# GpSimd's small indirect DMAs are handed out tile by tile in nine stages of a graph transformer

## The chip, the cores and the metric

One NeuronCore of one Trainium2 chip runs the whole program in one launch. The metric is device time in microseconds, from several runs of the same kernel. TensorE (PE), VectorE (DVE), ScalarE (ACT) and GpSimd (POOL) compute; SyncE (SP) and GpSimd issue DMAs, which sixteen DMA engines carry out.

## The reference, cut to what matters

3125 nodes with 256 features, 100,000 edges. Two blocks of layers:

```
xn = layernorm(x)
x  = x + graph_attention_2_layers(xn, src, dst) + hyperbolic_mixer(xn)      # block 0
x  = x + routed_mlp(layernorm(x))                                           # top half of the nodes
xn = layernorm(x)
x  = x + graph_convolution(xn, src, dst) + linear_attention_4_layers(xn)    # block 1
x  = x + experts(layernorm(x))      # 4 dense MLPs, mixed by gates
```

The gates of `experts` come from a small graph attention over 65,536 edges: for each edge, a row of 20 numbers of its source node is needed, and the edges must be sorted by destination. The kernel sorts them itself by a two-pass radix sort (by the low 6 bits, then by the high bits of the destination). Each pass ends in a scatter of 65,536 words of 4 bytes to memory, 128 words to a DMA, so 512 DMAs a pass. The fetch of the rows is 537 gathers of 128 rows of 80 bytes.

## The kernel before, in words

The nodes lie as 25 tiles of 125 rows (`NT = 25`, `P = 125`). The program is a sequence of *phases*; `phase` opens a block in which each engine gets its own list of instructions, ordered by semaphores alone, and a phase ends when every engine has finished its list and met at a barrier. What one engine has left to do is therefore waited for by all.

The small DMAs are independent of the work around them. They are put on GpSimd, which has little else to do, as a `side` of a phase. `Scatter.beside(count)` takes the next `count` of the 512 and issues them from the start of the phase one after another; `Scatter.send` waits only at every eighth, for the batch of eight that was sent two batches earlier to have landed. `Lookup.beside(e, ...)` issues the gathers of expert `e`, 136 in each of the first three and 129 in the last, without any wait. In the convolution (`Convolution.beside`) the same scatter DMAs are woven between gathers of 1.5 KB rows that do wait for their buffers.

The stages that the change touches, with the count of small DMAs beside each:

- `mix`, first product: 84 DMAs. Each of 25 tiles is scaled by ACT, turned and multiplied by PE (24 matmul instructions) and copied out by DVE. `made` counts the tiles that PE has finished; PE raises it by one at the start.
- `mix`, the mixer proper: 190 DMAs. Each tile goes PE, ACT, DVE and back twice; `out_ready` counts the tiles whose `attend` (L1483 is its last instruction) is done, and starts at one.
- `graph_attention_layer`, the projections to q, k and v (`tile_pass`), twice: 42 DMAs in layer 0 (behind the stores of `h` and `x`, and before `all_landed` and `load_steers`, five more DMAs and their wait), 80 in layer 1 (before `all_landed`). `down` counts tiles that PE has finished, from one.
- `routed_ffn`, the MLP by pairs of tiles (`pair_pass`): 130 DMAs. `up` counts quarters of the first product: 4 in each of 13 pairs, 52 in all, from zero.
- `experts`, four times `expert_mlp` (`tile_pass` with a `weave` of the edges' lookups on PE and DVE): 136, 136, 136 and 129 gathers. `down` counts tiles, from one.

Other scatter DMAs (12, 10, 42, 20, 16, 16 and 12, 40, 12 and those of block 1) stand beside phases that the change leaves alone, and nothing in these waits for a tile.

Of the kernel before, what the change touches and what calls it, by code (L numbers as in the profile page):

```python
# [14 lines left out]
N, D, E = 3125, 256, 100000  # L15
P = 125
NT = N // P
# [9 lines left out]
TAIL = 112  # L27
EC = 65536 // 128
# [31 lines left out]
def fetching(*sets):  # L60

    def side(block, s):
        @block.sync
        def _(sp):
            for fetch, pairs in sets:
                fetch.start(sp, pairs)
    return side


def together(*sides):  # L70

    def side(block, s):
        for one in sides:
            one(block, s)
    return side
# [5 lines left out]
@contextmanager  # L81
def phase(nc, g, *names):

    COUNT[0] += 1
    sems = [nc.alloc_semaphore(f"{n}_{COUNT[0]}") for n in names]
    with nc.Block() as block:  # L86
        yield block, dict(zip(names, sems))
    nc.clear_and_free_semaphores(sems)
    nc.all_engine_barrier()  # L89
# [16 lines left out]
def before(eng, sem, t, unit=1, more=0, light=False):  # L106


    (eng.wait_ge if light else hold_on(eng))(sem, (t + 1) * unit + more)


def this(eng, sem, t, unit=1, more=0, light=False):

    (eng.wait_ge if light else hold_on(eng))(sem, (t + 2) * unit + more)
# [22 lines left out]
def col(ap, t, width=1):  # L137

    return ap[:, bass.ds(t * width, width)]
# [301 lines left out]
def load_steers(nc, g, d, pool, done):  # L441

    nc.gpsimd.dma_start(g.wide_steer, d.steer[4:5, :]).then_inc(done, 16)
    for n, row in enumerate((g.pe_steer, g.act_steer)):
        for m in range(2):
            nc.gpsimd.dma_start(row.rearrange("a (k h j) -> a h k j", h=2, j=GG)[:, m],
                                d.steer[2 * n + m:2 * n + m + 1].rearrange("a (k j) -> a k j", j=GG)).then_inc(done, 16)
    pool.wait_ge(done, 16 * 5)
# [429 lines left out]
class Scatter:  # L878
# [41 lines left out]
    def beside(self, count):  # L920
        first = self.take(count)

        def side(block, s):
            @block.gpsimd
            def _(pool):
                self.send(pool, first, count)
        return side

    def close(self):
        self.nc.clear_and_free_semaphores(self.landed)  # L930
        self.nc.all_engine_barrier()
# [218 lines left out]
def split_k(dram, nk):  # L1150
    return dram.rearrange("(k p) n -> p k n", k=nk)


def w3(buf, nk, n):
    return buf[:, 0:nk * n].rearrange("p (k n) -> p k n", k=nk)
# [25 lines left out]
def mlp(nc, g, src, H, func, dst, coef, **more):  # L1181
    def finish(V, t, u, down):
        return V.scalar_tensor_tensor(col(dst, t, D), down[u], col(coef, t), col(dst, t, D), ALU.mult, ALU.add)

    pair_pass(nc, g, src, H, func, finish, **more)
# [15 lines left out]
def mix(nc, g, xn, x, w_qkv, gamma, beta, w_dw, w_pw, w_res, b_res, scatter, next_weights):  # L1201
# [9 lines left out]
    with phase(nc, g, "step", "squared", "summed", "rooted", "ready", "logged") as (block, s):  # L1211
        scatter.beside(10)(block, s)

        @block.scalar
        def _(act):
            nc.scalar.activation(g.b2, xn, ACT.Square).then_inc(s["squared"], 1)
            act.wait_ge(s["summed"], 1)
            nc.scalar.activation(nq, n2, ACT.Sqrt).then_inc(s["rooted"], 1)
            act.wait_ge(s["ready"], 1)
            nc.scalar.activation(za, n2, ACT.Ln, bias=1.0, scale=1.0)  # L1220
            nc.scalar.activation(zb, n2, ACT.Ln, bias=1.0, scale=-1.0).then_inc(s["logged"], 1)
# [20 lines left out]
    hT = g.ht[:, 0:2 * P].rearrange("p (k r) -> p k r", r=P)  # L1242

    with phase(nc, g, "loaded", "staged", "turned", "fetched", "made", "kept") as (block, s):
        scatter.beside(84)(block, s)

        @block.scalar
        def _(act):
            act.sem_inc(s["staged"], 1)
            with act.Fori(0, NT) as t:  # L1250
                before(act, s["turned"], t)
                nc.scalar.activation(g.stage[:, 0:D], col(xn, t, D), ACT.Copy, scale=col(s1, t)).then_inc(s["staged"], 1)

        @block.tensor
        def _(pe):
            pe.sem_inc(s["turned"], 1)
            pe.sem_inc(s["made"], 1)
            g.proj_w.wait(pe)
            with pe.Fori(0, NT) as t:
                this(pe, s["staged"], t)  # L1260
                for k in range(2):
                    ins = nc.tensor.transpose(psT[:, k, :], g.stage[:, k * 128:(k + 1) * 128], g.ident[0:P, 0:P])
                ins.then_inc(s["turned"], 1)
                this(pe, s["fetched"], t)
                before(pe, s["kept"], t)
                for j in range(6):
                    ps = psA[:, j, :] if j < 4 else psB[:, j - 4, :]
                    for k in range(2):
                        ins = nc.tensor.matmul(ps, g.w1[:, k * MIX + j * 128:k * MIX + (j + 1) * 128], hT[:, k, :],
                                               start=(k == 0), stop=(k == 1))  # L1270
                ins.then_inc(s["made"], 1)

        @block.vector
        def _(dve):
            dve.sem_inc(s["fetched"], 1)
            dve.sem_inc(s["kept"], 1)
            with dve.Fori(0, NT) as t:
                this(dve, s["turned"], t)
                before(dve, s["made"], t)
                nc.vector.tensor_copy(hT, psT).then_inc(s["fetched"], 1)  # L1280
                this(dve, s["made"], t)
                nc.vector.tensor_copy(H3[:, 0:4, bass.ds(t * P, P)], psA)
                nc.vector.tensor_copy(H3[:, 4:6, bass.ds(t * P, P)], psB).then_inc(s["kept"], 1)
# [59 lines left out]
    with ExitStack() as ctx:  # L1343
# [8 lines left out]
        oT = [w[:, 0:4 * P].rearrange("p (k r) -> p k r", r=P) for w in spare]  # L1352
        with phase(nc, g, "taken", "turned", "sq1", "nn1", "sq2", "nn2", "cat_ready", "sq3", "nn3", "out_ready",
                   "oturned", "ofetched", "made", "kept", "step1", "step2", "step3", "step4") as (block, s):
            scatter.beside(190)(block, s)

            def two_before(eng, sem, t):

# [186 lines left out]
def graph_attention_layer(nc, g, d, Wo, gam, bet, upcoming, scatter, first):  # L1545
# [4 lines left out]
    marks = {}  # L1550
    def side(block, s):
        marks["cut"] = s["side_a"]
        left = scatter.given
        scatter.take((EC - TAIL if first else EC) - left)

        @block.gpsimd
        def _(pool):
            moves = [(d.h_kept, g.h)] + ([(d.x_kept, g.x)] if first else [])
            g.proj_w.wait(pool)
            for dram, ap in moves:  # L1560
                nc.gpsimd.dma_start(dram, ap).then_inc(s["side_b"], 16)
            if not first:
                scatter.send(pool, left, EC - left)
                scatter.all_landed(pool)
            pool.wait_ge(s["side_b"], 16 * len(moves))
            if first:
                scatter.send(pool, left, EC - TAIL - left)
                scatter.all_landed(pool, EC - TAIL)
                scatter.saved.wait(pool)
                load_steers(nc, g, d, pool, s["steered"])  # L1570
# [60 lines left out]
    down = [g.ps[0:P, 4 + u, 0:D] for u in range(2)]  # L1631
# [363 lines left out]
def routed_ffn(nc, g, a, d, scatter):  # L1995
# [10 lines left out]
    def take(n):  # L2006
        at[0] += n
        return g.view(at[0] - n, n, P)
# [4 lines left out]
    cand, count, junk = take(16), take(16), take(16)  # L2013
    digit, less, many, base = take(1), take(1), take(1), take(2)
    cmp = take(16 * NT).rearrange("p (k t) -> p k t", t=NT)
    marks, through, zeros, tri = take(2 * NT), take(NT), take(NT), take(P)
    products, X3 = (b.rearrange("p (t n) -> p t n", t=NT) for b in (g.b2, xn))
    with phase(nc, g, "loaded", "step", "tri", "counted", "summed", "marked", "placed") as (block, s):
# [23 lines left out]
        def _(dve):  # L2042
# [20 lines left out]
            def search(key, at, first, n0):  # L2063
                step(V.memset(at, first))
                for n, size in enumerate((4096.0, 256.0, 16.0, 1.0)):
# [25 lines left out]
            step(V.tensor_tensor(g.coef[:, 0:NT], below, wt, ALU.mult))  # L2091
            step(V.tensor_tensor(x, x, xn, ALU.add))
    mlp(nc, g, xn, 1024, ACT.Gelu_apprx_tanh, x, g.coef[:, 0:NT], ready=[g.mlp_w, g.small_b],
        side=together(scatter.beside(130), fetching((g.conv_w, [(w3(g.cat[:, 0:512], 2, D), split_k(a["L1_gnn_W"], 2))]),
                                                    (g.proj_w, mixer_proj(g, a, 0)))))


def mixer_proj(g, a, l):
    return proj_weights(g.proj, [a["L1_mix_" + w][l] for w in ("Wq", "Wk", "Wv")])
# [458 lines left out]
class Lookup:  # L2558
# [39 lines left out]
    def beside(self, e, stores):  # L2598
        def side(block, s):
            @block.gpsimd  # L2600
            def _(pool):
                nc = self.nc
                if e == 0:
                    nc.gpsimd.memset(self.edges.rows[:, FILLED:TILES, 0:20], 0.0).then_inc(self.blank, 1)
                for t in self.rows_of(e):
                    nc.gpsimd.indirect_dma_start(self.edges.rows[:, t, 0:20], None, self.d.tab,  # L2606
                                                 bass.IndirectOffsetOnAxis(self.edges.src[:, t:t + 1], 0)).then_inc(self.got[e], 16)

            if not stores:
                @block.sync  # L2610
                def _(sp):
                    while self.fed < self.feeds_of(e):
                        self.feed(sp)
        return side
# [565 lines left out]
```

## Time and profile before

| what | value |
|---|---|
| median of 3 runs | 7761.05 us (7757.84 to 7766.31) |
| span of the profiled execution | 9096.7 us |
| PE busy in it | 5399.1 us (59%) |
| DVE busy in it | 4800.4 us (53%) |
| POOL busy in it | 4684.3 us (51%) |
| ACT busy in it | 2366.9 us (26%) |
| instructions | 106534 |

The three runs are timed without the profiler. The profiled execution has no time of its own in the results beside its span; the span, from first to last instruction, is 1335.65 us longer than the median. In the rows, a timeline line gives start, duration, engine, line, operation, tiles and, in brackets, the idle time before it with what ended it.

### The profile page before, as it was taken

How to read it: one execution, taken by the hardware profiler on the slowest of the kernel's cores; microseconds unless marked ns; L12 is line 12 of the kernel's file. 1: busy time of each engine (PE TensorE's matmuls, PEld its weight loads, DVE VectorE, ACT ScalarE, POOL GpSimd, SP SyncE). 2: the span in 40 equal slices, each digit the busy share in tenths (PEclk: the TensorE clock that was granted, in tenths of full speed). 3: DMA queues.
4: the chain of work that ended last, by engine and by line, in shares of the span. 5: the costliest groups of instructions: out<-in, count | busy, mean ns of one | idle time of the engine just before them, and what ended most of it. 6: DMA issues, size and time to landing. Idle time of an engine off the chain costs nothing. (4 is left out here: it accounts for less than half of the span.)

```text
span 9096.7 us, 106534 instructions
## 1 busy us (share of the span) xinstructions
PE 5399.1 (59%) x27548; PEld 4114.8 (45%) x27548; DVE 4800.4 (53%) x9729; ACT 2366.9 (26%) x6492; POOL 4684.3 (51%) x4114
## 2 busy tenths in 40 slices
PE   3312447777763677777653758859686871563353
PEld 1312335555543455555442536647474661452342
DVE  9124738888862787778580354454545450110047
ACT  0022314444541344444310211212122110110011
POOL 1363148777744777777025055757566545324500
PEclk9756679999987888888876879979798885776675
DMA  2000047777741776666100123414233331111101
GB/s 33 0 4 0 13 108 191 184 184 184 188 106 46 188 179 176 175 175 176 46 10 5 40 57 79 109 43 113 52 100 82 79 88 22 30 25 27 27 6 46
DMA packets 686839, 772.10 MB, mean 85 GB/s; under 512 B 470465, under 2 KB 515274, under 8 KB 685208
## 3 DMA queue, kind: packets, MB, share of 16 engines
q0 software_dynamic: 557488, 618.01, 28.3%
q1 hardware_dynamic: 128848, 147.93, 5.7%
q8 instruction: 249, 4.08, 0.2%
q14 instruction: 254, 2.08, 0.1%
HBM read 720.16 MB, written 42.74 MB: 84 GB/s over the span
## 5 line engine op out<-in xcount | busy, mean ns | idle before, releaser
L1711 POOL DMA_INDIRECT arena<-kv_rows,visit_src x1664 | 2055.8, 1235 | 793.9 <-issue 631.8
L2201 POOL DMA_INDIRECT arena<-piece_rows,visit_src x832 | 1022.5, 1229 | 640.7 <-PE ps L2263 325.5
L899 POOL DMA_INDIRECT sorted<-arena,cat x512 | 559.7, 1093 | 683.4 <-PEq L86 444.0
L1966 ACT CAST ps<-cat 125x265 bf16 x1664 | 637.8, 383 | 869.5 <-issue 412.7
L2606 POOL DMA_INDIRECT arena<-tab,visit_src x537 | 508.7, 947 | 586.0 <-POOLq L89 411.3
L899 POOL DMA_INDIRECT by_low<-steer x400 | 399.5, 999 | 759.3 <-PEq L86 596.5
L1867 PE MATMUL ps<-arena,w 125*125 x4992 | 753.4, 302 | 53.3 <-DVE stage L1753 39.4
L1867 PEld LDWEIGHTS ps<-arena,w 125*125 125x125 bf16 x4992 | 651.0, 142 | 185.1 <-issue 162.7
L1906 PE MATMUL ps<-arena,o 125*125 125x265 f32 x1664 | 596.4, 516 | 136.7 <-DVE ps L1823 63.8
L1906 PE MATMUL ps<-h,cat 125*125 125x265 f32 x1664 | 509.9, 421 | 234.2 <-issue 159.9
L1967 ACT COPY arena<-ps x1664 | 622.5, 374 | 0.5
L823 PE MATMUL ps<-ht,w 128*128 128x250 f32 (+1 forms) x2496 | 565.1, 380 | 87.2 <-issue 68.9
L698 DVE COPY ht<-ps 128x250 f32<-128x250 f32 x350 | 143.9, 411 | 883.6 <-DMA piece_rows<-o 556.8
L647 PE MATMUL ps<-ident,stage 125*128 125x125 f32 x900 | 206.5, 314 | 628.0 <-ACT stage L602 364.3
L2282 DVE TENSOR_TENSOR arena<-arena,ps 125x256 f32 x832 | 350.2, 421 | 355.8 <-PE ps L2263 217.5
L823 PEld LDWEIGHTS ps<-ht,w 128*128 128x128 f32 x2496 | 469.5, 198 | 149.5 <-issue 86.5
L1906 PEld LDWEIGHTS ps<-arena,o 125*125 125x125 f32 x1664 | 380.3, 245 | 276.0 <-issue 199.6
L796 ACT ACTIVATE h<-ps,vec 128x250 f32<-128x250 f32 (+1 forms) x468 | 189.8, 458 | 1065.6 <-PE ps L823 740.6
L1906 PEld LDWEIGHTS ps<-h,cat 125*125 125x125 f32 x1664 | 273.2, 189 | 421.1 <-issue 396.9
L837 PE MATMUL ps<-w,h 128*125 128x256 f32 x1800 | 426.2, 386 | 37.2 <-issue 19.0
L1753 DVE TENSOR_TENSOR stage<-arena,ps 125x512 f32<-125x512 f32 x416 | 285.3, 686 | 278.3 <-PE ps L1867 160.2
L647 PEld LDWEIGHTS ps<-ident,stage 125*128 125x128 f32 x900 | 109.6, 155 | 694.2 <-ACT stage L602 339.2
(589 smaller groups left out, 10802.3 us busy)
## 6 DMA issues: line engine op xcount, KB each, us to landing
w<-rel SPq DMA_DIRECT2D x104, 488.3 KB
arena<-kv_rows,visit_src POOLq DMA_INDIRECT x1664
arena<-rel SPq DMA_DIRECT2D x34, 512.0 KB
arena<-piece_rows,visit_src POOLq DMA_INDIRECT x832
kv_rows<-h SPq DMA_DIRECT2D x50, 250.0 KB
x_kept<-arena POOLq DMA_DIRECT2D x3, 3125.0 KB
arena<-tab,visit_src POOLq DMA_INDIRECT x537
sorted<-arena,cat POOLq DMA_INDIRECT x512
```

The lines of the kernel that those rows point to most:

```text
L647: ins = nc.tensor.transpose(psT_[u][:, k, :], stage_[u][:, k * 128:(k + 1) * 128], g.ident[0:P, 0:P])
L823: ins = nc.tensor.matmul(up(j)[:, 0:n * P], g.w1[:, k * H + j * 128:k * H + (j + 1) * 128], hT[:, k, 0:n * P], start=(k == 0), stop=(k == 1))
L837: nc.tensor.matmul(down[u], h1[j][:, u * P:(u + 1) * P], g.w2[:, j * D:(j + 1) * D], start=(j == 0), stop=False)
L899: self.nc.gpsimd.indirect_dma_start(self.rows, bass.IndirectOffsetOnAxis(self.places[:, c - self.base:c - self.base + 1], 0), self.values[ ...
L1711: nc.gpsimd.indirect_dma_start(ring[k % RG][:, j, :], None, d.kv, bass.IndirectOffsetOnAxis(g.srcv[:, v:v + 1], 0)).then_inc(got[k % RG], 16)
L1867: ins = nc.tensor.matmul(psQ[n][:, j * D:(j + 1) * D], ohT[b % 4][:, e:e + P], q[:, bass.ds(at[2 * n + j], D)], start=(m == 0), stop=(m == 2))
L1906: nc.tensor.matmul(flat[0:P, bass.ds(at[j], WIDE)], oh[k % 2][:, j * P:(j + 1) * P], ms[k % 2][:, j, :], start=False, stop=True, skip_grou ...
L1966: nc.scalar.copy(flat[0:P, bass.ds(clean[j], WIDE)], zeros[:, 0:WIDE]).then_inc(s["zeroed"], 1)
L1967: nc.scalar.copy(g.sums_all[:, bass.ds(home[j], WIDE)], flat[0:P, bass.ds(bank[j], WIDE)]).then_inc(s["evicted"], 1)
L2201: nc.gpsimd.indirect_dma_start(self.rows[v % (self.RG * GG)], None, self.d.pieces, bass.IndirectOffsetOnAxis(g.srcv[:, v:v + 1], 0)).then_ ...
L2282: dve.tensor_tensor(at, at, c.bank[q % 2][:, j * D:(j + 1) * D], ALU.add).then_inc(c.added, 1)
L2606: nc.gpsimd.indirect_dma_start(self.edges.rows[:, t, 0:20], None, self.d.tab, bass.IndirectOffsetOnAxis(self.edges.src[:, t:t + 1], 0)).th ...
```

## The change

`Scatter.along` replaces `Scatter.beside` in four places, and `send_along` replaces `send` in the two layers of graph attention. Both cut the DMAs into as many shares as there are marks, and GpSimd waits ahead of share n until the given semaphore has reached mark n. In `Lookup.beside` the gathers are cut into 25 shares, and share k (from 1 on) waits for `down` to be k + 1, which is k finished tiles. The number, order, addresses and data of the DMAs stay, and so do all other engines' instructions.

```diff
+    def send_along(self, pool, first, count, progress, marks):
+        sent = 0
+        for n, mark in enumerate(marks):
+            due = count * (n + 1) // len(marks)
+            if due > sent and mark:
+                pool.wait_ge(progress, mark)
+            self.send(pool, first + sent, due - sent)
+            sent = due
+
+    def along(self, count, progress, marks):
+        first = self.take(count)
+        def side(block, s):
+            @block.gpsimd
+            def _(pool):
+                self.send_along(pool, first, count, s[progress], marks)
+        return side
 ...
-        scatter.beside(84)(block, s)
+        scatter.along(84, "made", range(1, NT + 1))(block, s)
 ...
-            scatter.beside(190)(block, s)
+            scatter.along(190, "out_ready", range(1, NT + 1))(block, s)
 ...
             if not first:
-                scatter.send(pool, left, EC - left)
+                scatter.send_along(pool, left, EC - left, s["down"], range(1, NT + 1))
                 scatter.all_landed(pool)
             pool.wait_ge(s["side_b"], 16 * len(moves))
             if first:
-                scatter.send(pool, left, EC - TAIL - left)
+                scatter.send_along(pool, left, EC - TAIL - left, s["down"], range(1, NT + 1))
                 scatter.all_landed(pool, EC - TAIL)
 ...
-        side=together(scatter.beside(130), fetching(...
+        side=together(scatter.along(130, "up", range(0, 4 * (NT + 1) // 2)), fetching(...
 ...
-                for t in self.rows_of(e):
+                mine, put = self.rows_of(e), 0
+                for n, t in enumerate(mine):
+                    if n * NT // len(mine) > put:
+                        put = n * NT // len(mine)
+                        pool.wait_ge(s["down"], put + 1)
                     nc.gpsimd.indirect_dma_start(self.edges.rows[:, t, 0:20], None, self.d.tab, ...
```

## Rows read from the trace of the kernel before

**Rows 1.** The page's first line: span and instructions of the profiled execution.

```profile
span 9096.7 us, 106534 instructions
```

**Rows 2.** The page's costly groups: small DMAs on GpSimd, count, busy us, mean ns, idle before.

```profile
L899 POOL DMA_INDIRECT sorted<-arena,cat x512 | 559.7, 1093 | 683.4 <-PEq L86 444.0
L2606 POOL DMA_INDIRECT arena<-tab,visit_src x537 | 508.7, 947 | 586.0 <-POOLq L89 411.3
```

**Rows 3.** Stretches: length, busy us (instructions) of PE PEld DVE ACT POOL, PEclk, DMA, GB/s.

```profile
260.00:365.00 105.00, 5.75 (x29) 5.25 (x27) 2.75 (x6) 1.01 (x2) 69.83 (x73) 0.53 0.02 0
375.00:470.00 95.00, 59.67 (x496) 55.75 (x496) 26.57 (x60) 9.64 (x19) 0.00 (x0) 1.00 0.00 0
550.00:776.00 226.00, 21.65 (x102) 18.27 (x101) 39.08 (x62) 16.66 (x36) 172.39 (x177) 0.55 0.02 1
820.00:1060.00 240.00, 126.08 (x514) 103.77 (x514) 195.73 (x335) 90.93 (x197) 0.00 (x0) 0.71 0.00 0
2781.00:2862.00 81.00, 12.05 (x35) 9.31 (x36) 3.98 (x10) 1.93 (x6) 61.34 (x64) 0.56 0.05 9
2885.00:2944.00 59.00, 51.46 (x236) 39.82 (x236) 32.68 (x85) 15.69 (x50) 0.00 (x0) 1.00 0.25 74
4814.00:4952.00 138.00, 23.05 (x44) 12.01 (x44) 0.88 (x2) 2.27 (x6) 103.86 (x109) 0.51 0.02 0
4984.00:5119.00 135.00, 135.00 (x632) 113.16 (x631) 13.99 (x27) 35.04 (x89) 0.00 (x0) 1.00 0.00 1
7565.00:7719.00 154.00, 16.93 (x61) 10.48 (x60) 1.50 (x3) 2.28 (x7) 114.33 (x121) 0.50 0.12 12
7742.00:7849.00 107.00, 107.00 (x946) 88.53 (x944) 23.69 (x58) 31.37 (x101) 0.00 (x0) 0.98 0.09 31
1400.00:2600.00 1200.00, 881.30 (x4146) 631.61 (x4144) 1005.37 (x1929) 591.17 (x1883) 940.10 (x759) 0.91 0.74 186
5600.00:5800.00 200.00, 199.10 (x1112) 171.92 (x1110) 89.38 (x207) 43.78 (x107) 156.82 (x132) 1.00 0.44 112
```

**Rows 4.** The timeline inside the burst of the routed MLP, PE and POOL.

```profile
4843.54 0.96 POOL L899 DMA_INDIRECT sorted<-arena,cat  x1 [0.30 <-issue]
4844.34 0.57 PE L823 MATMUL ps<-ht,w 128*128 128x250 f32 x1 [2.23 <-issue]
4844.80 0.96 POOL L899 DMA_INDIRECT sorted<-arena,cat  x1 [0.30 <-issue]
4845.74 0.29 PEld L823 LDWEIGHTS ps<-ht,w 128*128 128x128 f32 x1 [2.51 <-issue]
4847.14 0.57 PE L823 MATMUL ps<-ht,w 128*128 128x250 f32 x1 [2.23 <-issue]
```

**Rows 5.** The timeline of the experts: first gather, first tile, tiles 20 apart, last stage's first gather.

```profile
7549.95 1.01 POOL L2606 DMA_INDIRECT arena<-tab,visit_src  x1 [0.49 <-issue]
...
7556.71 0.69 PE L674 MATMUL ps<-brow,ones 1*125 1x256 f32 x2
...
7746.64 0.42 DVE L1160 COPY arena<-ps 125x256 f32<-125x256 f32 x1 [3.38 <-PE ps L674]
...
7848.94 0.43 DVE L1160 COPY arena<-ps 125x256 f32<-125x256 f32 x1 [1.93 <-PE ps L674]
...
8480.06 0.95 POOL L2606 DMA_INDIRECT arena<-tab,visit_src  x1 [142.51 <-POOLq L89]
8481.31 0.95 POOL L2606 DMA_INDIRECT arena<-tab,visit_src  x1 [0.30 <-issue]
```

**Rows 6.** The timeline of layer 1's projections: the store of `h`, and the first tile's cast.

```profile
2759.57 0.61 POOL L1561 DMA_DIRECT2D h_kept<-arena  x1 [3.04 <-POOLq L89]
...
2766.94 0.42 DVE L1575 CAST arena<-ps 125x256 f32 x1 [4.24 <-PE ps L672]
```

**Rows 7.** The timeline at the mixer's end: the last tile but one attended, the last tile kept.

```profile
1069.68 0.69 DVE L1483 TENSOR_TENSOR w<-w 125x512 f32<-125x512 f32 x1
...
1085.31 0.48 DVE L1491 SCALAR_TENSOR_TENSOR arena<-ps,cat,w 125x256 f32<-125x256 f32 x1 [4.14 <-PE ps L1393]
```

More of the change, by code:

```diff
@@ L2093, in routed_ffn @@
     mlp(nc, g, xn, 1024, ACT.Gelu_apprx_tanh, x, g.coef[:, 0:NT], ready=[g.mlp_w, g.small_b],
-        side=together(scatter.beside(130), fetching((g.conv_w, [(w3(g.cat[:, 0:512], 2, D), split_k(a["L1_gnn_W"], 2))]),
+        side=together(scatter.along(130, "up", range(0, 4 * (NT + 1) // 2)), fetching((g.conv_w, [(w3(g.cat[:, 0:512], 2, D), split_k(a["L1_gnn_W"], 2))]),
                                                     (g.proj_w, mixer_proj(g, a, 0)))))
```

## The prediction

> **What bounds the kernel now.** I read four views: the page's head against the runs' times, the table of stretches, the timeline inside one burst, and the timeline at the ends of the stages.
>
> The head first, because it is the oddest number here. The profiled execution's span is 9096.7 us [rows 1] and the median without the profiler 7761.05 us: 1335.65 us, 17%, more. So a duration in this trace need not be one of the timed runs, and the first question is where the 1336 us lie.
>
> The stretches come in pairs [rows 3]: first one in which GpSimd issues small DMAs back to back, then one of the same stage when it is done. In the first product of `mix` PE issues 29 instructions in 105 us of burst and 496 in 95 us after it. In the mixer it is 102 in 226 us against 514 in 240, in layer 1's projections 35 in 81 against 236 in 59, in the routed MLP 44 in 138 against 632 in 135, with the experts 61 in 154 against 946 in 107. DVE and ACT all but stand too, and the granted clock is 0.50 to 0.56 in the bursts. In the trace, then, the bursts stop the core. The small DMAs of these stages are 84 + 190 + 42 + 80 + 130 scatters and all 537 gathers, 1063 in all; the 512 scatters of a pass are busy 1093 ns each and the gathers 947 [rows 2], and within a burst they follow at intervals of 1.26 us (4844.80 less 4843.54, [rows 4]) and 1.25 us (8481.31 less 8480.06, [rows 5]).
>
> What stops it is no work. Inside a burst PE takes one instruction every 1.40 us, a matmul at 4844.34, a weight load at 4845.74, a matmul at 4847.14, each released by nothing that the profile shows ("issue") [rows 4]. The DMA engines are 2% busy there. GpSimd is busy for 75% of that stretch (103.86 of 138 us); in the convolution it is busy for 78% (156.82 of 200) beside 44% of the DMA engines, and PE is busy for 199 of 200 us at full clock; in edge attention likewise 78% beside 74%, and nothing stands [rows 3]. What is higher in the bursts is only how many descriptors start: 109 DMAs of 128 in 138 us is 101 a microsecond, against 759 of 125 in 1200 us, 79, and 132 of 125 in 200 us, 83. Something that takes a small, fixed toll of each descriptor and each instruction fills up between 83 and 101. The profiler's recording is such a thing, and the timed runs have none.
>
> The Trainium skill says that the notification block's internal pipeline holds its producers back rather than lose a record ("NOTIFIC — the notification-queue block", 7.1, on overflow). The even 1.40 us of PE agree with it; no row here shows the block itself. By this rule the stalls belong to the profiled execution alone.
>
> **How much of the gap the stalls are.** I turn the instructions issued in each burst into time at the pace after it [rows 3]. `mix` 1: 29/496 of 95 us is 6, so 99 of 105 us are lost. Mixer: 102/514 of 240 is 48, 178 lost. Layer 1's projections: 35/236 of 59 is 9, 72 lost. Routed MLP: 44/632 of 135 is 9, 129 lost. Layer 0's 42 DMAs by layer 1's rate, 72 for 64: some 45, of which I take 35 since the stores of `h` and `x` stand ahead. For the experts I count by stage: three take 8480.06 less 7549.95, 930 us, so 310 each [rows 5]. Free of stalls a tile takes (7848.94 less 7746.64)/20 = 5.1 us, 25 tiles 128 us; but 136 gathers at 1.25 us take 170, so GpSimd would bind at 170 plus some 3 for the phase's turn. Lost: 137 in each, 548 in four. Sum: 99 + 178 + 72 + 129 + 35 + 548 = 1061 us of the 1336.
>
> The other 275 are 3.4% of the remaining 8036 us. Could they be much more, so that the stalls were real and something else gave the gap? Hardly: the convolution's stretches can't shrink, since PE is full at full clock; edge attention has DVE busy for 1005 of 1200 us, so at the very best 16% shrink there. To find 1336 us outside the bursts one would need 17% everywhere.
>
> **The change part by part.** It removes nothing and adds waits on GpSimd: 24 or fewer in eight stages, 51 in the routed MLP.
>
> *Beside tiles slower than GpSimd.* Per tile, `mix` 1 needs 84/25 x 1.26 = 4.2 us of GpSimd against 5.0 us of tile (26 PE instructions, 496 in 95 us). The mixer needs 9.6 against 14.0 (30, 514 in 240). The routed MLP needs 12.6 per pair against 15.0 (70, 632 in 135). Here the waits spread the DMAs, and only the last share counts, as it starts when the last tile but one is marked. In the mixer that is 8 DMAs, 10.1 us, from 1070.37; the last tile is kept at 1085.79 [rows 7], so 5 us to spare. In `mix` 1 it is 4 DMAs, 5.0 us, beside a tile of 5.0; in the MLP 3 DMAs, 3.8 us, beside GELU and second product. I take 0.
>
> *Beside tiles faster than GpSimd.* Layer 1's projections need 3.2 x 1.26 = 4.0 us against 3.5 (14 instructions, 236 in 59 us); an expert's tile 5.44 x 1.25 = 6.8 against 5.1. In the timed runs GpSimd sets these ends already, at 101 and 170 us against 88 and 128 of tiles, and every us that it waits is added whole. It waits only at the start. The projections' first share is 3 DMAs, ending near 2760.2 + 3.8 = 2764.0; the first tile's cast starts at 2766.94 [rows 6]: 2.5 us lost. An expert's is 6 gathers, 7549.95 + 7.5 = 7557.45, and the first tile is down at 7556.71 + 0.69 = 7557.40 [rows 5]: 0, at most 1 a stage; I take 1 for four. Queued behind these waits are `all_landed` in the projections, and nothing else; SP and the rel feeds don't pass through GpSimd.
>
> *Layer 0's projections.* The 42 DMAs begin behind the stores as before, but the last 2 now start beside the last tile, and `all_landed` and the five DMAs of `load_steers` behind them: 2.5 + 5 x 0.61 (the store's time on GpSimd, [rows 6]) and two landings, against one tile of 3.5 us and its own store. Bound 0 to 8; I take 3.
>
> *A wait that is already met.* No row of its own; below nothing it can't go. The nearest are the 0.30 us of "issue" ahead of each small DMA, with or without one of `send`'s waits [rows 4, 5]. I take 0; at 0.05 us each in the 4 x 24 + 24 that GpSimd's end hangs on, 6 us is the upper bound.
>
> The sum for timed runs: 2.5 + 1 + 3 = 6.5 us, so 7767 us, no change that can be told (0.2%, 15.5 us, is about what a measurement of this kernel tells from none). Against the profiled execution's own span the sum is another: 9096.7 - 1061 + 6.5, about 8042 us, if spreading ends the stalls. In the projections and the experts GpSimd runs on without rest, so some stalling may stay until its own wait stops it: 7950 to 8400.
>
> **The rivals.**
>
> *The stalls are real, in part or whole.* For it: they are the largest losses in sight, and GpSimd's DMAs do land in memory that all share. Against it: the gap, and the idle DMA engines. Whole: 7761 less 1061, 6700 us. A quarter: 7496. Each tenth is 106 us. It decides from the smallest real share, 2%. The skill states that the profile's total and the reported execution time differ by a constant 6.2 us ("Runtime: NRT & Kernel Launch", the launch sequence). By that rule the trace would be the timed run and this rival whole; 9096.7 against 7761.05 says otherwise. I give 20%: 3 whole, 11 below 7700, 6 in between.
>
> *The last shares stand behind the last tiles* (slower). If GpSimd is quicker without the profiler, the experts become bound by tiles, and the ends of nine stages each carry a share: 4 + 8 + 2 + 4 + 3 = 21 scatters at 1.26 and 20 gathers at 1.25, 51.5 us, with `load_steers` and a landing 57: 7818 us. It decides where less than the share's 2.5 to 10 us remains after the mark; one expert tile of 5.1 covers all but 1.2 of 6.3 us, and the mixer covers all. 14%, and mostly 16 to 40 us.
>
> *The change doesn't spread.* In experts and projections each mark is met before GpSimd comes to it. Then the bursts stay in the trace (span near 8660) and timed runs stay at 7767. Inside the likeliest case, a tenth of it.
>
> **How the numbers follow.** No change 66%, faster 20%, slower 14%; predicted 7767. The range 7700 to 7800 leaves out some 14% below and 4% above. The likeliest case's own range is 7755 to 7776.
>
> **What would show it.** In the trace of the changed kernel: the mixer's tiles 14 us apart from the first on, its stage near 360 us instead of 550; the routed MLP near 200; PE's 1.40 us steps gone there; an expert's stage 170 to 200 us instead of 310; the span some 1000 us nearer to the timed runs while these stay put. A wait of GpSimd for PE of 2 to 3 us early in layer 1's projections and none later in the experts. Wrong would be a median under 7745, which makes the stalls real, or over 7777 with phases ending on GpSimd's last share.

## The result, and the profile after

| | median (us) | runs |
|---|---|---|
| before | 7761.05 | 7757.84 to 7766.31 |
| after | 7792.40 | 7786.96 to 7800.60 |

The ratio is 1.004, its 95% interval 1.0027 to 1.0052: 31.35 us slower. The forecast was 7767, 25.4 us less. The measured time lies in the range given (7700 to 7800), but outside the likeliest case's own range (7755 to 7776); of the cases told apart beforehand the slower one (14%), "the last shares stand behind the last tiles, mostly 16 to 40 us", names the size.

The page of the changed kernel begins so (its line answers to [rows 1]):

```profile
span 7792.0 us, 106555 instructions
...
PE 5229.5 (67%) x27548; PEld 4014.7 (52%) x27548; DVE 4793.7 (62%) x9729; ACT 2365.5 (30%) x6492; POOL 4693.2 (60%) x4114
```

The gap is gone: the span is 1.7 us short of the same execution's 7793.71 us, where the span of before was 1335.65 over the median. PE's busy time is down from 5399.1 us and POOL's is 9 us more. The stretches beside the small DMAs (columns as in [rows 3]; mix's first product, mixer, layer 1's projections, routed MLP, experts, edge attention):

```profile
245.00:360.00 115.00, 74.38 (x611) 69.69 (x611) 30.56 (x69) 11.68 (x23) 73.69 (x77) 0.99 0.02 0
440.00:765.00 325.00, 159.87 (x699) 130.01 (x697) 266.46 (x452) 121.47 (x263) 175.67 (x178) 0.74 0.01 0
2375.00:2470.00 95.00, 71.20 (x318) 55.23 (x317) 46.02 (x117) 21.26 (x67) 66.38 (x70) 0.93 0.29 77
4215.00:4395.00 180.00, 180.00 (x836) 150.78 (x835) 19.18 (x38) 47.86 (x120) 114.48 (x120) 0.99 0.02 2
6765.00:6890.00 125.00, 124.25 (x1074) 103.09 (x1073) 27.75 (x65) 36.57 (x118) 93.33 (x98) 0.98 0.25 55
1400.00:2200.00 800.00, 600.52 (x2873) 433.46 (x2873) 690.64 (x1328) 409.90 (x1306) 642.45 (x518) 0.91 0.77 191
```

Tiles and small DMAs run beside each other, at a granted clock of 0.93 to 0.99 (near 2.4 GHz) and 0.74 in the mixer. In [rows 3] mix's first product had 29 PE instructions in 105 us at a clock of 0.53; here it has 611 in 115 us. This looks like the change's work. It is not: the first experiment shows the unchanged kernel doing the same.

### The profile page after: what moved, and what is told of

Its sections match the earlier page's. It is cut to its first block and busy times, and to the rows that moved or that the text cites. A ratio compares the mean times of both kernels' runs of the same rounds, so it can differ in the third digit from the quotient of the medians.

```text
span 7792.0 us, 106555 instructions
## 1 busy us (share of the span) xinstructions
PE 5229.5 (67%) x27548; PEld 4014.7 (52%) x27548; DVE 4793.7 (62%) x9729; ACT 2365.5 (30%) x6492; POOL 4693.2 (60%) x4114
## 5 line engine op out<-in xcount | busy, mean ns | idle before, releaser
L1925 PE MATMUL ps<-arena,o 125*125 125x265 f32 x1664 | 564.5, 495 | 136.1 <-DVE ps L1842 75.4
L1925 PEld LDWEIGHTS ps<-arena,o 125*125 125x125 f32 x1664 | 358.8, 233 | 266.8 <-issue 200.9
```

The costliest lines, as they stand in the source:

```text
L1925: nc.tensor.matmul(flat[0:P, bass.ds(at[j], WIDE)], oh[k % 2][:, j * P:(j + 1) * P], ms[k % 2][:, j, :], start=False, stop=True, skip_grou ...
```

## The experiments

### The kernel before, profiled again

> The kernel before, unchanged, profiled again. Theory A (the stalls of the bursts come and go with the recording of one execution): its time is 7761 us again, and the profiled span is either near that, with the mixer stage at about 350 us and an expert stage at 173 us, or stalled once more near 9100; in both cases the time of the runs stays. Rival B (the stalls are part of the kernel and the runs time something else): the span is 9097 us within 1% and no run is near it. Where the span is near 7760 this trace is the base for all stage lengths.

Measured: 7753.75 us. Its page's first line, then the same kind of stretches (the first five stages inside their small DMAs, and edge attention):

```profile
span 7752.0 us, 106534 instructions
```

```profile
245.00:345.00 100.00, 64.64 (x530) 60.56 (x529) 26.57 (x60) 10.15 (x20) 75.91 (x80) 0.99 0.02 0
...
440.00:675.00 235.00, 134.09 (x526) 112.15 (x527) 192.78 (x328) 88.75 (x190) 180.12 (x181) 0.63 0.02 1
...
2365.00:2450.00 85.00, 67.53 (x304) 52.74 (x304) 42.25 (x109) 20.52 (x64) 64.66 (x67) 0.94 0.27 72
4190.00:4345.00 155.00, 155.00 (x726) 130.16 (x725) 15.55 (x30) 43.43 (x109) 117.66 (x123) 1.00 0.02 1
6735.00:6860.00 125.00, 124.30 (x1072) 102.76 (x1071) 27.76 (x65) 36.51 (x118) 94.83 (x100) 0.98 0.24 53
1400.00:2200.00 800.00, 597.79 (x2848) 430.61 (x2847) 689.85 (x1332) 406.31 (x1296) 642.50 (x518) 0.91 0.76 190
```

In 100 us of mix's first product PE issues 530 instructions beside 80 small DMAs. So the stalls are no part of the kernel, as Theory A had it. All of the 1345 us between this span and 9096.7 were of that one execution. Phase by phase (each phase ends in a clearing of its semaphores on GpSimd, so the two traces can be laid side by side) it lost 102 us in mix's first product, 203 in the mixer, 42 and 79 in the projections, 156 in the routed MLP, 526 in the experts: 1108, where the prediction worked out 1061. Edge attention lost 152 more, the rest lay in phases with other scatters. None of the eleven other profiled executions shows such stalls, and of the 59 timed executions of this kernel whose spans are on record none is over 7773.8 us. Why they came in the one no run here shows. The Trainium skill's rule on backpressure ("NOTIFIC — the notification-queue block", 7.1) says no more than that such stalls can be.

This trace is the base of all that follows. It is a quick execution, 9.5 us under the median of this kernel on the same chip (7763.25). The next table gives each phase's length in it and by how much it differs in the other profiled runs (us; single executions). "All" is the changed kernel; the other columns are the experiments below, in their order: waits in the projections, in the experts, in mix, mixer and MLP ("slow" tiles) only; all waits three tiles earlier; the store in mid-stage; all one tile later; DMAs moved; the store of `h` in pieces in layer 1, and in both layers.

```
                     base   all  proj.  exp.  slow 3early store 1late moved pieces  both
mix, first product  127.3  +5.7  +0.6  -0.2  +8.0  -0.4  +5.9 +11.2  +2.2  +2.2  +0.3
mixer               348.9  +0.9  -0.6  +0.1  +0.6  -0.5  +0.9 +11.3  +0.5  +0.5  -1.1
layer 0 projections 122.3  +5.6  +4.5  -0.3  +0.2  +0.5  +3.5  +6.7  +1.0  +0.5  -5.1
edge attention 1   1326.7  -0.6  -1.4  +1.1  +1.1  +9.5  +6.8  +5.7  +4.5  +7.0  +6.7
layer 1 projections 112.2  +9.1  +9.7  +0.6  +0.7  +2.4 +11.7 +13.6  -6.3 -14.5 -11.8
edge attention 2   1319.7  +5.3  +1.3  +7.4  +3.9  +0.9  +2.1  +2.7  +4.7  +1.3  +3.2
routed MLP          193.5  +5.0  +0.8  +0.8  +6.0  +0.1  +6.0  +5.4  +0.6  +0.3  -0.0
experts, four       701.8  +9.6  +3.1  +9.1  +1.6  +3.8  +7.2 +29.1  +2.9  +2.0  +1.6
all others         3499.8  -0.6  -1.0  +0.2  -4.4  -4.5  -3.4  -5.5  -2.3  -6.8  -5.3
```

Edge attention, which no kernel changes, wanders by up to 9.5 us from one execution to another, so a span alone tells little. The phases that the change touches wander less where nothing in them is changed: mix's first product is -0.2 to +2.2 us off the base, the mixer, the projections and the MLP -0.6 to +0.8. The experts without waits are 0 to 3.1 over the base, 1.9 in the mean of six.

### Waits in one kind of stage only

Three kernels, each with a part of the change and the rest as before: the two projection stages; the experts; mix's first product, mixer and routed MLP. The first as a diff against the changed kernel:

```diff
-        scatter.along(84, "made", range(1, NT + 1))(block, s)
+        scatter.beside(84)(block, s)
 ...   (likewise 190 and 130)
-                        pool.wait_ge(s["down"], put + 1)
```

> Only the two projection stages have the waits (42 and 80 DMAs); the mixer, the routed MLP and the experts have none. Theory A (GpSimd sets the end where tiles are faster than it, so every us it waits for tiles is added; in layer 1 the second tile is held by the 3.2 MB store of h in front of the kv rows, and GpSimd idles 3.1 + 7.7 us there): 12 to 20 us slower than before, so 7773 to 7781. Rival B (the cost is in the stages with slow tiles, by last shares behind last tiles): 0 to 5 us slower, 7761 to 7766.

> Only the experts' gathers have the waits. Theory A: GpSimd binds all four stages at 170 us and waits early in each (0.6 + 2.2 us, and more with cold tiles, in the first of the changed kernel), so 8 to 16 us slower than before, 7769 to 7777. Rival B: within 4 us of before, 7757 to 7765.

> Only the stages whose tiles are slower than GpSimd have the waits: the first product of mix, the mixer and the routed MLP. Theory A: the last shares are covered, 0 to 4 us slower than before, 7761 to 7765. Rival B (last shares stand behind the last tiles, or the spread DMAs slow each tile): 15 to 30 us slower, 7776 to 7791.

| waits in | median (us) | ratio to before | 95% interval |
|---|---|---|---|
| projections | 7785.55 | 1.0031 | 1.0019 to 1.0043 |
| experts | 7768.86 | 1.0008 | 0.9999 to 1.0017 |
| mix, mixer, routed MLP | 7771.41 | 1.0012 | 1.0003 to 1.0021 |

The excesses by these ratios, 24, 6 and 9 us, sum to 39 against 31 for the whole, within the intervals. Theory A's figures were all missed: the projections are above its 7773 to 7781, the experts just below its 7769 to 7777 and not clear of zero, the slow tiles between its 7761 to 7765 and B's 7776 to 7791. The medians alone therefore do not settle it; the table of phases does. Each part costs in its own phases what it costs in the changed kernel: the two projections 14.2 us (14.7; the profiled execution is the quickest of its six, 7770.75, and the other 8 us of the median are not explained), the experts 9.1 (9.6). The slow tiles cost more than Theory A gave them: 5.7 to 8.0 us at the end of mix's first product, 5.0 to 6.0 in the routed MLP. In mix the changed kernel's timeline reads:

```profile
361.04 0.95 POOL L899 DMA_INDIRECT by_low<-steer  x1 [1.23 <-PE ps L1288]
...
364.82 0.96 POOL L899 DMA_INDIRECT by_low<-steer  x1 [0.31 <-issue]
...
366.53 0.41 DVE L1302 COPY arena<-ps 128x250 f32 x1
...
374.34 0.96 POOL L899 DMA_INDIRECT by_low<-steer  x1 [8.56 <-PEq L86]
```

The last share is the four DMAs foreseen, done at 365.78, before the last tile (366.94). But the next phase's first DMA comes 8.56 us later: GpSimd's own end of phase lasts until 372.74, 7.0 us behind its last DMA and 5.8 behind the last tile. In the base this tail ran beside tiles: the last DMA ended at 346.94 and GpSimd then stood for 21.55 us until the tiles had ended. The mixer is alike (last DMA done at 775.78, GpSimd at its end 782.58, last tile 780.89), but there only 1.7 us stand behind the last tile. The routed MLP ends in another way:

```profile
4382.81 0.96 POOL L899 DMA_INDIRECT sorted<-arena,cat  x1 [2.69 <-PE ps L823]
...
4396.79 0.96 POOL L899 DMA_INDIRECT sorted<-arena,cat  x1 [1.40 <-PE ps L823]
...
4405.62 0.96 POOL L899 DMA_INDIRECT sorted<-arena,cat  x1 [0.30 <-issue]
4410.22 0.96 POOL L899 DMA_INDIRECT sorted<-arena,cat  x1 [3.64 <-PEq L86]
```

The last pair is a single tile, and PE runs through its four quarters in 3.84 us. Eight DMAs, not three, stand behind the last binding wait: done at 4406.58, where the last tile was kept at 4403.41.

### The same waits, three tiles earlier

```diff
-        scatter.along(84, "made", range(1, NT + 1))(block, s)
+        scatter.along(84, "made", [0] * 3 + list(range(1, NT - 2)))(block, s)
```

and so in the other stages (a mark of zero is no wait).

> All waits of the change, but each asks for three tiles less (six quarters less in the routed MLP), so GpSimd keeps its waits and its spreading and gets a lead. Theory A (what is added is the time that GpSimd stands in binding waits, plus the tail behind its last DMA where that comes out after the tiles): no wait binds where GpSimd sets the end (in layer 1's projections 25 DMAs at 1.26 us reach the tile that held it at 30.4 us after 31.5 us), and the last share of mix's first product starts 3 x 4.9 us earlier, more than the 5.8 us it was late. So every stage has the length of before, within 1 us, and the median is 7763, within 4. Rival C (a wait costs by itself, or spreading the DMAs does): the some 250 waits are still there and so is the time, 10 us or more over before; at 0.1 us for each of the 24 waits of the six stages that GpSimd ends it would be 14 us. Rival B of the first runs (last shares behind the last tiles) expects the same here as A.

Measured: 7763.58 us, ratio 0.9998 (0.9989 to 1.0007). Every stage is back within 0.5 us of the base but layer 1's (+2.4, with one wait of 1.01 us for the scatters' own landings) and the experts, at +3.8 within or near the spread without waits. Rival C, 10 us or more, is out: waits that are met, and DMAs spread over tiles, cost nothing that can be told, 5 us at most by the interval.

### One tile later

```diff
-        scatter.along(84, "made", range(1, NT + 1))(block, s)
+        scatter.along(84, "made", range(2, NT + 2))(block, s)
```

> All of the change, and each share waits for one tile more (not in the routed MLP). Theory A, stage by stage over the changed kernel: mix's first product one tile, 4.9; the mixer 10 to 13; layer 0's projections 3 to 4; layer 1's 3.5; each of four experts one tile, 5.1, so 20. Sum 42 to 46, a median near 7836. Rival C (cost of the waits themselves or of spreading): the same number of waits, so it stays near 7792. If only the stages with slow tiles mattered, the experts would add nothing: 7811.

Measured: 7838.69 us, ratio 1.0097 (1.0081 to 1.0112), 46 over the changed kernel where 42 to 46 were expected. By phases, over the changed kernel: 5.5 us in mix's first product, 10.4 in the mixer, 1.1 and 4.5 in the projections of layers 0 and 1, 19.5 in the experts; only layer 0 is off what was expected, 3 to 4. With the last experiment this is a dose and its answer: by the lead that GpSimd has over its tiles the cost goes from none over 31 to 75 us.

### The large store in mid-stage

Layer 1's projections of the changed kernel, POOL:

```profile
2363.89 0.61 POOL L1580 DMA_DIRECT2D h_kept<-arena  x1 [3.04 <-POOLq L89]
2364.81 1.00 POOL L899 DMA_INDIRECT by_low<-w  x1 [0.30 <-issue]
...
2371.40 0.96 POOL L899 DMA_INDIRECT by_low<-w  x1 [3.07 <-PE ps L672]
...
2395.21 0.96 POOL L899 DMA_INDIRECT by_low<-w  x1 [7.71 <-PE ps L672]
```

The first wait is the one foreseen (2 to 3 us). The second was not: PE is late because its copies out wait for the stores of earlier tiles, and these stand behind the 3125 KB of `h`. Base and changed kernel have such a row (11.36 us in the changed one); the base's is

```profile
2373.84 0.37 ACT L1582 COPY h<-ps 125x256 f32<-125x256 f32 x1 [11.80 <-DMA kv_rows<-h]
```

In the base GpSimd runs past it. To test it, the store moved behind the twelfth share:

```diff
+                scatter.send_along(pool, left, early, s["down"], range(1, 13))
+                nc.gpsimd.dma_start(*moves[0]).then_inc(s["side_b"], 16)
+                scatter.send_along(pool, left + early, EC - left - early, s["down"], range(13, NT + 1))
```

> All of the change, but GpSimd issues the 3125 KB store of h in layer 1's projections after its twelfth share and not ahead of the first. Theory A: the 7.7 us wait there comes from tiles held by their own stores behind that of h, so it goes; the first wait (3.1 us) stays; the store now holds two tiles by some 10 us in mid-stage, of which GpSimd, 6 us behind the tiles by then, feels 4. Layer 1's stage, 9.1 us over before with the change, falls to 3 to 7 over, and the median from 7792 to 7786 to 7790. Rival D (the tiles are late in this place for another reason, the turn of the phase or the weights): the 7.7 us wait stays where it is and the stage stays at 9 over.

Measured: 7799.53 us, ratio 1.0045 (1.0032 to 1.0059), the stage 11.7 over the base: a miss. Its POOL timeline:

```profile
2375.49 0.96 POOL L899 DMA_INDIRECT by_low<-w  x1 [2.65 <-PE ps L672]
2395.73 0.96 POOL L899 DMA_INDIRECT by_low<-w  x1 [0.30 <-PE ps L672]
2419.46 0.61 POOL L1585 DMA_DIRECT2D h_kept<-arena  x1
...
2440.14 0.96 POOL L899 DMA_INDIRECT by_low<-w  x1 [7.39 <-DMA by_low<-w]
2450.22 0.96 POOL L899 DMA_INDIRECT by_low<-w  x1 [2.79 <-PE ps L672]
```

The 7.7 us wait is gone, so its cause was named rightly. But the store now lies ahead of scatters for whose landing `send` waits at every eighth: 7.39 us, and 2.79 for a held tile behind it. One wait took the place of another.

### Small DMAs moved to where there is room

The base shows GpSimd done with the mixer's DMAs 100 us before the mixer ends. This run is the kernel before, without any wait, with layer 1's 80 small DMAs put beside the mixer and layer 0 (`TAIL` is how many of the 512 are left behind layer 0):

```diff
-TAIL = 112
+TAIL = 32
 ...
-            scatter.beside(190)(block, s)
+            scatter.beside(260)(block, s)
```

> The kernel before, without waits, with the 80 small DMAs of layer 1's projections put elsewhere: 70 more stand beside the mixer (260 in place of 190), 10 more beside layer 0's projections (52 in place of 42). In the trace of before without stalls GpSimd is done with the mixer's at 676 of 776 us, and layer 1's tiles are done some 8 us before GpSimd's end of phase. Theory A (GpSimd, its DMAs and the tail behind them, set the end of layer 1's projections): that stage falls from 112.2 to 103 to 106 us, mixer and layer 0 stay within 1.5 us, and the median is 6 to 9 us under before, near 7756. Rival (the tiles and their stores set it): 0 to 2 us under. Against both, if 260 DMAs don't fit beside the mixer, it is slower there.

Measured: 7760.95 us beside 7763.95 for before, ratio 0.9994 (0.9985 to 1.0003). The stage fell to 105.9 us, as expected, and so GpSimd and its tail did set its end. The median is 3 us under before where 6 to 9 were expected, and it can't be told from no change, nor from the 6 us; in the profiled execution other phases were longer (table).

Next, on top of this, `h` in 25 pieces that are handed out by tiles, in layer 1; then in layer 0 too, there without waits, each piece followed by its share of the 52 small DMAs, behind the landing of `x`. The edit in layer 1:

```diff
-            for dram, ap in moves:
-                nc.gpsimd.dma_start(dram, ap).then_inc(s["side_b"], 16)
+            for t in range(NT):
+                if t:
+                    pool.wait_ge(s["down"], t + 1)
+                nc.gpsimd.dma_start(d.h_kept[:, t * D:(t + 1) * D], g.h[:, t * D:(t + 1) * D]).then_inc(s["side_b"], 16)
```

> As the kernel with 80 small DMAs moved out of layer 1's projections (7760.95), and there the 3125 KB store of h is cut into 25 pieces of a tile, of which piece k waits for k finished tiles. The large store and not the small DMAs is now handed out. Theory A (the store ahead of the tiles' own stores holds tiles 2 and 3 by some 10 us, and with the small DMAs gone the tiles set the end): the stage falls from 105.9 to 96 to 99 us and the median is 7751 to 7754, some 10 under before. Rival (the same bytes cost the tiles the same time wherever they go): 104 to 107 us and 7761.

> As the last one, and in layer 0's projections h goes in 25 pieces too, each followed by its share of the 52 small DMAs, without waits; only x (3125 KB) still goes first and whole. Layer 0's stage, 123.3 us, is tiles held by stores: with one large store less ahead, some 10 us less of holding, but GpSimd now has 52 x 1.26 + 25 x 0.6 = 81 us from the landing of x on (some 20 us in), 5 us of steers and a tail of up to 8: 114 to 118 us. So 5 to 9 us less than the last kernel, 7743 to 7748. Rival (GpSimd's longer list sets the end, or the bytes cost the same): 122 to 125 us, no gain.

| `h` in pieces in | median (us) | ratio to before (7755.65 on that chip) | layer 0 / layer 1 stage (us) |
|---|---|---|---|
| layer 1 | 7746.32 | 0.9987 (0.9978 to 0.9996) | 122.8 / 97.7 |
| both | 7738.48 | 0.9973 (0.9961 to 0.9985) | 117.2 / 100.4 |

The stages' lengths came as expected (96 to 99 us in layer 1, 114 to 118 in layer 0), and so did the differences: 9 us under before, and 8 less again. The medians lie 5 us under the figures given, which had reckoned from another chip's 7761. The second kernel is 17 us faster than before by the medians and beats both kernels. With pieces the tile's copy waits 3.35 us where it waited 11.80:

```profile
2376.43 0.37 ACT L1586 COPY h<-ps 125x256 f32<-125x256 f32 x1 [3.35 <-DMA kv_rows<-h]
```

## Why the prediction was right, and where its sum was not

The range 7700 to 7800 held, but that is in part luck: the likeliest case's sum has 6.5 us where 31 were measured, and what it named as a sign of being wrong, a median over 7777 with phases that end on GpSimd's last share, is what came. The time lies in the range by the room that was left for the slower rival.

**The gap.** Right: the stalls were the profiled execution's alone, and 1061 us for the nine stages stand against 1108 measured. Wrong was the span given for the changed kernel, 8042 (7950 to 8400): it took the other 275 us for something that would stay, and edge attention at 78% was thought undisturbed. It had lost 152 us. Not the change but another execution ended the stalls. The cause given for them, something that fills up between 83 and 101 descriptors a microsecond, is not borne out: the first experiment has 80 DMAs of 128 in 100 us, 102 a microsecond, in a profiled execution too, and nothing stands. Nor is it shown that the timed runs have no recording: a span and a granted clock are on record for each timed execution of the changed kernel and of the experiments. The rival "the stalls are real" (20%) fell with the first experiment. Between a span and the reported time of the same execution lie 1.7 to 1.8 us here, the time being the longer. The Trainium skill states that the profile's total is the longer, by some 6.2 us ("Runtime: NRT & Kernel Launch", the launch sequence); whether it means this span, from first to last instruction, no run here shows.

**Beside slower tiles: taken at 0, measured 0.9 in the mixer, 5.7 in mix, 5.0 in the MLP.** The shares in mix and the mixer were counted rightly. The step that failed is the comparison of the last DMA's end with the last tile's ("5 us to spare" in the mixer, which measured 5.1; "4 DMAs, 5.0 us, beside a tile of 5.0" in mix): it left out what GpSimd needs behind its last DMA, 7.0 us in mix and 6.8 in the mixer. In the MLP "3 DMAs, 3.8 us" took the last mark to be a quarter of a full pair; the last pair has one tile, and 8 DMAs stand behind it.

**Beside faster tiles: taken at 2.5 + 1, measured 9.1 + 7.7** (9.6 less the 1.9 of experts without waits). That GpSimd sets these ends and that binding waits are added nearly whole is what the runs bear out: in layer 1 the two waits, 3.07 and 7.71 us, are 10.2 over the 0.30 that stands before each DMA anyway, and the last DMA comes 9.6 us later in the phase. "It waits only at the start" failed: the sum took the tile's pace as even. In layer 1 the tiles stop for 9 to 12 us behind a store, and the second wait comes from it; without waits they took 103 us in the base, not the 88 of the sum. In the experts GpSimd stood for PE seven times, 9.4 us in all. The first of the four shows it, its second tile being later than 5.1 us behind the first:

```profile
6770.00 0.94 POOL L2629 DMA_INDIRECT arena<-tab,visit_src  x1 [0.57 <-PE ps L674]
...
6778.38 0.94 POOL L2629 DMA_INDIRECT arena<-tab,visit_src  x1 [2.16 <-PE ps L674]
```

**Layer 0: taken at 3, measured 5.6.** Inside the bound of 8. The tiles are paced by their stores here (in the base ACT waited 75.0 us for them, in 21 waits), and behind the last binding wait, which ends at 931.93, come four DMAs, their landing, the steers and GpSimd's end of phase: it ends at 950.5, 9.3 us after the last tile's last instruction (941.2).

**A wait already met: 0**, borne out by the kernel with three tiles less.

**The rivals.** The slower one was told as one share behind each last tile, 51.5 us in all, if GpSimd were quicker than in the trace; it was not (one DMA in 1.26 us as before). Two stages of the nine did that (mix, MLP), for 11 us; the larger part, 22 us, was lost in binding waits that the likeliest case had, under-sized. The terms measured sum to 34 us (0.9 + 5.7 + 5.0 + 9.1 + 7.7 + 5.6) against the medians' 31.

**Open:** why one profiled execution stalled; and what moves edge attention by up to 9.5 us between executions of the same instructions.

## What to carry to other kernels

A wait that only spreads another engine's work is free where that engine has a lead, and costs its full length where that engine sets the stage's end; size it by the most uneven tiles of the stage, not by the mean pace, and add what the engine needs behind its last DMA. A lead of three tiles made all these waits free, as far as can be told. If one execution's span is far from the timed runs, take a second one before reading any stall in it; and where one large store stands ahead of the tiles' own, as here, it is that one which is worth cutting up.

## What the runs showed of the hardware

- Behind its last small indirect DMA GpSimd took 7.0 us to the end of its phase in mix's first product, 6.8 in the mixer, but 2.2 in the routed MLP and 2.4 to 3.1 in the experts. In mix and the MLP it is the same within 0.1 us in all eleven traces without stalls, spread DMAs or not; in the mixer it is 6.8 with 190 DMAs and 3.4 in the three kernels with 260. What makes it long or short wasn't tried.
- A 3125 KB store from GpSimd held GpSimd's own 4-byte scatters and SyncE's 250 KB stores alike: 7.39 us for the ones, 9 to 12 us for the others. With two such stores ahead, in layer 0 of the base, a tile's copy waited up to 24.4 us.
- One profiled execution ran 1345 us longer than another of the same kernel, with PE at one instruction every 1.40 us beside small DMAs [rows 4].
